# Cross attention: the context rows turned by VectorE from a second load instead of by TensorE

## What is computed

```python
def xattn(x, z, Wq, Wkv, Wo):          # x: 64 x 32 x 512, z: 64 x 257 x 256, 16 heads of 32
    Q = (x @ Wq.T).reshape(B, xN, 16, 32)
    KV = (z @ Wkv.T).reshape(B, zN, 2, 16, 32)
    K, V = KV[:, :, 0], KV[:, :, 1]
    attn = softmax(einsum('bqhd,bkhd->bhqk', Q, K) * SCALE, axis=-1)
    O = einsum('bhqk,bkhd->bqhd', attn, V).reshape(B, xN, 512)
    return O @ Wo.T
x = x + xattn(layernorm(x), ctx_512, ...)
```

## Time and profile before

| | |
|---|---|
| median of 3 runs | 1498.38 us (1495.2 to 1499.29) |
| span of the profiled execution | 1492.9 us, 39481 instructions |
| TensorE busy | 1434.5 us, 96% |
| VectorE busy | 1088.6 us, 73% |
| ScalarE busy | 807.5 us, 54% |
| GpSimd busy | 543.6 us, 36% |
| mean granted clock of TensorE | 0.990 |

### The profile page before, as it was taken

The page is one execution under the profiler, slowest core; times in us unless marked ns, Lnnn a source line. Parts: engine busy times, 40 slices in busy tenths (PEclk is TensorE's granted clock), DMA queues, the critical chain, the costliest instruction groups (busy, mean ns, idle before and its releaser), DMA issues. The chain is left out here.

```text
span 1492.9 us, 39481 instructions
## 1 busy us (share of the span) xinstructions
PE 1434.5 (96%) x14944; PEld 1281.3 (86%) x14944; DVE 1088.6 (73%) x1945; ACT 807.5 (54%) x1525; POOL 543.6 (36%) x810
## 2 busy tenths in 40 slices
PE   7999999999999999998999998799999999999998
PEld 6888888988888888887778786698999999999997
DVE  3676777767777677776667686797887878787785
ACT  4666666666666666654434434345555545555452
POOL 1222222221222222224866876453333333333232
PEclk9999999999999999999999999899999999999999
DMA  6301101000001100100011014179877878787871
GB/s 239 125 28 31 30 22 29 29 22 29 22 28 28 29 28 23 30 9 1 31 38 38 32 38 155 57 220 314 281 263 247 286 253 267 262 279 238 292 256 44
DMA packets 130734, 174.11 MB, mean 117 GB/s; under 512 B 16953, under 2 KB 89337, under 8 KB 130626
## 3 DMA queue, kind: packets, MB, share of 16 engines
q1 hardware_dynamic: 120242, 145.56, 30.1%
q0 software_dynamic: 10384, 27.05, 5.0%
HBM read 157.18 MB, written 19.06 MB: 118 GB/s over the span
## 5 line engine op out<-in xcount | busy, mean ns | idle before, releaser
L2229 DVE TENSOR_TENSOR split<-raw,split 128x1024 fp32r<-128x1024 f32 x204 | 242.3, 1220 | 7.2 <-ACT split L2169 6.0
L52 PE MATMUL bank<-split_xT,split 128*128 128x256 f32 x768 | 216.5, 282 | 0.4 <-DVE split L2229 0.2
L54 PE MATMUL bank<-split_xT,split 128*128 128x256 f32 x768 | 215.4, 281 | 0.0
L53 PE MATMUL bank<-split_xT,split 128*128 128x256 f32 x768 | 215.4, 280 | 0.0
L2169 ACT CAST split<-raw 128x1024 fp32r<-128x1024 f32 x202 | 203.2, 1048 | 6.9 <-DMA raw<-in_L_ffn_W_dram 3.2
L596 ACT ACTIVATE Pr<-xa_s,nmax 128x257 f32<-128x257 f32 x256 | 118.7, 473 | 124.9 <-DVE nmax L696 124.8
L2189 ACT ACTIVATE sl<-bank 128x256 f32<-128x256 f32 x115 | 44.2, 384 | 240.8 <-PE bank L54 223.5
L52 PE MATMUL xa_s<-split,split 128*128 128x258 f32 x512 | 150.5, 294 | 1.9 <-DVE split L628 1.9
L52 PEld LDWEIGHTS bank<-split_xT,split 128*128 128x128 f32 x768 | 144.9, 189 | 7.0 <-issue 2.8
L53 PEld LDWEIGHTS bank<-split_xT,split 128*128 128x128 f32 x768 | 145.0, 189 | 3.1
L53 PE MATMUL xa_s<-split,split 128*128 128x258 f32 x512 | 145.6, 284 | 0.0
(11 more groups left out here) (317 smaller groups left out, 3915.1 us busy)
## 6 DMA issues: line engine op xcount, KB each, us to landing
raw<-in_L_ffn_W_dram SPq DMA_DIRECT2D x207, 512.0 KB
raw<-in_ctx_dram SPq DMA_DIRECT2D x64, 256.0 KB, 2.6
out_dram<-x_res SPq DMA_DIRECT2D x16, 256.0 KB
xs<-xn SPq DMA_DIRECT2D x16, 256.0 KB
x_res<-in_x_dram SPq DMA_DIRECT2D x1, 3584.0 KB, 18.7
VL<-v_last_rows SPq DMA_DIRECT2D x128, 2.0 KB, 1.5
raw_o<-in_L_xattn_Wo_dram SPq DMA_DIRECT2D x1, 1024.0 KB, 6.4
raw_q<-in_L_xattn_Wq_dram SPq DMA_DIRECT2D x1, 1024.0 KB, 9.5
```

The lines of the kernel that those rows point to most:

```text
L52: pe.matmul(out, lh, rh, start=start, stop=False)
L53: pe.matmul(out, ll, rh, start=False, stop=False)
L54: return pe.matmul(out, lh, rl, start=False, stop=stop)
L2229: vW.done(dve.tensor_tensor(lo, raw, hi.bitcast(F32), ALU.subtract), f"p{c}{q}")
```

## The change

z comes to the core a second time, in 32x32 blocks. `load_blocks` brings a sequence in four transfers of 128-byte runs, so that the block of 32 keys and 32 features stands with its keys on the 32 partitions where its features shall end. VectorE then turns the blocks within each group of 32 partitions by two block transposes of 128x256 (`turn_z`, now on VectorE), into an SBUF buffer `zT`. `z_hi` and `z_lo` read `zT` instead of PSUM, and TensorE's turns are gone. The blocks have two buffers and `zT` one; they lie in the third weight slot. The weights of the self attention that were loaded there (wv, wo) are loaded at the end of the cross attention, each with a semaphore of its own that ScalarE waits for.

The transposes write whole runs of 32 keys, which makes the keys stand in another order along a row; `load_z` gives the rows of z the same order, in four transfers of 64 KB. The transposes stand on VectorE behind the second maximum (at j=0 also behind the masked copies, at j=2 behind the layer norm) and ahead of the reciprocal. The diff's core:

```diff
+        GRP = P // HD
+        zb = [lent.w2[:, n, :] for n in range(2)]
+        zb_got = [sem(f"zb_got{n}") for n in range(2)]
+        zT = lent.w13[:, 1, 0:2].rearrange("p k w -> p (k w)").rearrange("p (k c) -> p k c", k=KL)
+        def load_blocks(sp, s, n):
+            blocks = ctx_in[s, 0:LAST, :].rearrange("(i n) (k g e) -> i g (n k) e", i=HD, k=KL, e=HD)
+            for g in range(GRP):
+                sp.dma_start(zb[n][g * HD:(g + 1) * HD, :].rearrange("p (n e) -> p n e", e=HD), blocks[:, g]).then_inc(zb_got[n], 16)
+        def turn_z(dve, n, got, s):
+            dve.wait_ge(zb_got[n], got)
+            if not isinstance(s, int) or s:
+                dve.wait_ge(a_T, s)
+                dve.wait_ge(v_T, s)
+            for k in range(KL):
+                dve.transpose(zT[:, k].rearrange("p (c b i) -> p b c i", c=CH, b=BT),
+                              zb[n].rearrange("p (b c k e) -> p k b c e", b=BT, c=CH, k=KL)[:, k]).then_inc(v_ZT, 1)
         def load_z(sp, s, j):
-            sp.dma_start(z_in[j], ctx_in[s, 0:LAST, :].rearrange("(p c) l -> p c l", c=CH)).then_inc(z_got[j], 16)
+            rows = ctx_in[s, 0:LAST, :].rearrange("(i b c) l -> b i (c l)", i=HD, b=BT)
+            for b in range(BT):
+                sp.dma_start(z_in[j][b * HD:(b + 1) * HD].rearrange("p c l -> p (c l)"), rows[b]).then_inc(z_got[j], 16)
...
-                    for j in range(BT):
-                        load_z(sp, j, j)
+                    load_blocks(sp, 0, 0)
+                    load_z(sp, 0, 0)
+                    load_z(sp, 1, 1)
+                    load_blocks(sp, 1, 1)
...
                         if not first:
-                            sp.wait_ge(pe_T, s - BT + 1)
                             sp.wait_ge(g_Z, s - BT + 1)
                             load_z(sp, s, j)
+                        elif j >= 2:
+                            load_z(sp, s, j)
+                        if not (last and j >= 2):
+                            sp.wait_ge(v_ZT, KL * s + KL)
+                            load_blocks(sp, s + 2, j % 2)
...
+                sp.wait_ge(v_T, s_end)
+                weights.load_v(sp)
+                weights.load_o(sp)
...
-                        if not (last and j == BT - 1):
-                            turn_z(s + 1, (j + 1) % BT, i + (j + 1) // BT)
...
                 def z_hi(s):
-                    act.wait_ge(pe_T, s + 1)
-                    act.copy(zT_hi[:, :, 0:LAST], bank_z[:].rearrange("p (k q) -> p k q", k=KL)).then_inc(a_T, 1)
+                    act.wait_ge(v_ZT, KL * s + KL)
+                    act.copy(zT_hi[:, :, 0:LAST], zT).then_inc(a_T, 1)
...
-                    dve.tensor_tensor(zT_lo[:, :, 0:LAST], bank_z[:].rearrange("p (k q) -> p k q", k=KL),
+                    dve.tensor_tensor(zT_lo[:, :, 0:LAST], zT,
                                       zT_hi[:, :, 0:LAST].bitcast(F32), ALU.subtract).then_inc(v_T, 1)
...
                         if j == 2:
                             normalise(dve, i + 2)
+                        if not (last and j == BT - 1):
+                            turn_z(dve, (j + 1) % 2, 16 * GRP * (2 * i + (j + 1) // 2 + 1), s + 1)
                         dve.wait_ge(a_E, 4 * s + 4)
                         dve.reciprocal(rinv[:], rsum[:]).then_inc(v_R, 1)
...
                 high(0)
+                act.wait_ge(w.v_got, 16)
                 w.high(act, 2)
...
+                act.wait_ge(w.o_got, 16)
                 w.high(act, 3)
```

More of the change, by code:

```diff
@@ L82, in block_constants, with cross_attention @@
     return ident
-def cross_attention(nc, x_in, ctx_in, Wq, Wkv, Wo, x_res, ident, vlast_dram, spare,
+def cross_attention(nc, x_in, ctx_in, Wq, Wkv, Wo, x_res, ident, vlast_dram, spare, lent,
                     spare_x, held, weights, beside):
@@ L312, in cross_attention @@
         vl_got, vl_made, vl_split = sem("vl_got"), sem("vl_made"), sem("vl_split")
-        pe_T, pe_S, pe_PT, pe_U, pe_QK = (sem(n) for n in ("pe_T", "pe_S", "pe_PT", "pe_U", "pe_QK"))
+        pe_S, pe_PT, pe_U, pe_QK = (sem(n) for n in ("pe_S", "pe_PT", "pe_U", "pe_QK"))
         pe_PL, pe_O, pe_Q, pe_OP = (sem(n) for n in ("pe_PL", "pe_O", "pe_Q", "pe_OP"))
@@ L679, in add_residual @@
                     dve.tensor_tensor(x_res[:, i, :], bank_o[:], x_res[:, i, :], ALU.add).then_inc(v_OP, 1)
+                turn_z(dve, 0, 16 * GRP, 0)
                 z_lo(0)
@@ L745, in split_z @@
                 def split_z(s, j, i):
-                    pool.wait_ge(z_got[j], 16 * i + 16)
+                    pool.wait_ge(z_got[j], 16 * BT * i + 16 * BT)
                     need(pool, pe_U, s)
@@ L822, in __init__ @@
         self.got = ctx.enter_context(nc.semaphore("sa_w_got"))
+        self.v_got, self.o_got = (ctx.enter_context(nc.semaphore(n)) for n in ("sa_wv_got", "sa_wo_got"))
         self.loads = [(dst, src.rearrange("(k p) c -> p k c", p=P)) for dst, src in (
-            (self.q, wq), (self.down[:], w_down), (self.k, wk_up), (self.v, wv_up), (self.o, wo), (self.router[:], Wr))]
+            (self.q, wq), (self.down[:], w_down), (self.k, wk_up), (self.router[:], Wr))]
+        self.late_v, self.late_o = ((dst, src.rearrange("(k p) c -> p k c", p=P)) for dst, src in ((self.v, wv_up), (self.o, wo)))
         self.loads.append((self.rope[:], rope.rearrange("p (a d) -> p a d", a=2)))
@@ L842, in load, with load_v, load_o @@
             sp.dma_start(dst, src).then_inc(self.got, 16)
+    def load_v(self, sp):
+        sp.dma_start(*self.late_v).then_inc(self.v_got, 16)
+    def load_o(self, sp):
+        sp.dma_start(*self.late_o).then_inc(self.o_got, 16)
     def wait(self, eng):
@@ L2405, in perceiver_block @@
             cross_attention(nc, x.rearrange("b t c -> (b t) c"), ctx_512, xWq, xWkv, xWo, x_res, ident,
-                            v_last, slots[0], xg, held, weights, clear_slots)
+                            v_last, slots[0], slots[2], xg, held, weights, clear_slots)
             banks = Banks(nc, ctx)
```

4 lines of the change are left out of this document (2 added, 2 removed).

## The result

The changed kernel takes 1483.26 us (median of four runs, 1483.19 to 1484.38) against 1498.84 us for the kernel before (1495.20 to 1500.59): a ratio of 0.990, with an interval of 0.989 to 0.992. The forecast was 1483.0 us. The profiled execution took 1484.38 us, with a span of 1482.6 us against 1492.9 before.

The account below looks back on a forecast made before the run. TensorE's own work was taken to bound the cross attention. The loop's -16.1 us and the start's +0.5 gave -15.6, so 1498.4 became 1482.8, say 1483 us; range 1471 to 1497, with 1480 to 1488 at 0.60.

Parts of the forecast that it names:

- The loop: Cross attention tiles: -1.14 us for each of 13 middle tiles (-14.8), with tiles 0, 14 and 15 summing to -16.1.
- j=0: Sequence without a VectorE gap: U ends 0.68 us later, the values wait, 11.22 against 11.04 us, a loss of 0.18.
- the list of signs: What would show the forecast right, including TensorE waiting near 0.9 us for VectorE's U ahead of the values at j=0.
- The pair: Two 128x256 block transposes per sequence on VectorE: 0.42 us each, 0.68 on its path with overlap.
- the rival of slow transposes: VectorE transposes at the 128x512 price: pair 1.28 us instead of 0.68, about 5 us lost, 1493; chance 0.14.
- The step that j=3 would pay from 1.2 us on: VectorE at j=3: with cover gone, each 0.1 us of the pair over 1.2 costs 0.1.
- The start: SyncE ahead of the first barrier: twelve more issues at 0.6 to 0.96 us each, put at +0.5 us, range 0 to +4.
- Loads in the loop: SyncE and DMA engines: eight 64 KB loads per sequence instead of one of 256 KB, and late wv and wo, cost nothing.
- The rival of late blocks: The eight loads exceed a sequence; each us over 10 adds to each of 62 sequences, 1545 at 11 us; chance 0.07.
- The shared path: VectorE's low half of z and GpSimd's split block each other; z_lo wins, the split runs 0.5 us late, harmlessly.
- The rival's mechanism: GpSimd's split, if issued first, makes z_lo wait 2 us: +2.9 a tile, +38 in all, 1536; chance 0.09.
- The baseline: The median 1498.4 us from which -15.6 was subtracted, with 2 to 6 us taken to lie around the profiled span.

Follow-up runs that it names:

- e1_start: The changed kernel with only the first sequence's block load ahead of the first barrier, the other loads issued behind it: 1478.03 us.
- e7_loads4: The kernel before with the new loads, blocks read by nothing, TensorE still turning z, rows of z loaded four sequences ahead: 1503.47 us, recorded ratio 1.0035.
- e5_pool: The changed kernel with GpSimd allowed to begin its split of z's rows one step earlier, issued ahead of VectorE's low part of z: 1486.47 us.
- e4_early: The changed kernel with the transposes at j=0 moved to the end of j=3 of the tile before, behind the low part of z: 1479.78 us.
- e3_double: The changed kernel with each pair of transposes done twice, first into a buffer that nothing reads: 1496.83 us.

## Why the prediction came out right, point by point

- **The loop** (forecast -16.1, profile -18.1 with -16.5 in tiles 1 to 13). Every turn that was to be won at j=1, j=2 and j=3 was won. Tile 0 gave -0.85 (forecast -0.9), tile 14 -0.94 (-0.7), and the first three sequences of tile 15 +0.21 (+0.3). What follows them to the self attention took 1.2 us more, where the granted clock fell (0.77 and 0.81 from 662 to 670 us); in e1_start the same code at full clock took what it took before.
- **j=0** (forecast +0.18 each, measured +0.04 on average). The mechanism was right: no gap, U late, TensorE waits 0.60 us for it (the list of signs said 0.9, the sum's own numbers make 8.43 - (8.08 - 0.44) = 0.79). The size was off by 0.14: U ends at 8.25 and not 8.38, since the pair follows the masks with 0.08 overlap and the reciprocal takes 0.14 us behind a transpose instead of 0.18.
- **The pair** (forecast 0.42 each, 0.68 on the path). Measured 0.418 and 0.68. Strided reads cost nothing; the rival of slow transposes is out. The step that j=3 would pay from 1.2 us on was too strict: with 1.33 us it paid 0.04 instead of 0.13.
- **The start** (forecast +0.5, at most +4; measured +7.25). This is the step that failed, in two ways. The sum priced twelve more issues at 0.6 to 0.96 us and left the first four at their old 3.82 us. The twelve took 6.9 us, 0.57 each, but the first four, now transfers of 128-byte runs, took 7.80 in the same place. So SyncE ended at 23.01, the upper end of the 19 to 23 that the prediction worked out, while the +0.5 came from near the lower end, and TensorE's start in the kernel before was 18.99 and not 19.7: 4.5 us. And the clock was put at nothing: the longer wait for the barrier was followed by a slower granted clock, 2.7 us. A first barrier several us later stood among the signs of being wrong, and it came.
- **Loads in the loop** (forecast nothing). Shown by e7_loads4, to 0.05 us in 525. The rival of late blocks is out: in the changed kernel's trace the transposes are idle ahead of them once only, at the first barrier, and ScalarE doesn't stand for wv or wo.
- **The shared path.** GpSimd's first instruction waits as forecast (0.57 instead of 0.19 us), L647 stays at 0.68. The rival's mechanism was right. Its condition was not enough, as GpSimd came first in one sequence of four though it was issued ahead in all, and its price was too high (e5_pool).
- **The baseline.** I subtracted from a median whose spread I had not explained. The 2 to 6 us that I put around the span are 1.7 to 2.3. The profiled pair says -18.1 + 7.25 + 1.2 - 0.7, which is -10.3; the two pairs of medians say -15.6 and -11.6. The loop's underestimate and the draw covered the start's error, and that is why 1483.0 met 1483.3: the total was luck, the loop's mechanism was not.

## What to carry to other kernels

When work goes from the engine that bounds to one with gaps, walk the gaps step by step: it was free in three of four sequences and cancelled its whole gain in the fourth, which had no gap. Count every DMA that is issued ahead of a barrier at the price of its own form, and put there only what the first step needs. Before a difference of a few microseconds is explained, learn what the kernel's own runs differ by, and where.

## What the runs showed of the hardware that was not expected

- In the changed kernel an issue of 64 KB in 512 runs of 128 bytes took SyncE 1.95 us on average (1.3 to 2.7) in the first four, while the start's weights were landing, 0.65 in the four at 19.77 us, and 0.57 at the median over all; one of z's rows of the same size took 0.53 at the start and 0.32 at the median.
- VectorE stands 0.21 us for nothing that the profile shows, ahead of the maxima at j=0 of the first tile of a pair, in five iterations of the hardware loop of pairs. Each time a branch of the loop (COMPARE_BRANCH, here at 354.34) stands 0.5 us before in VectorE's own queue:

```profile
354.83 1.29 DVE L716 TENSOR_REDUCE nmax<-xa_s 128x2 f32<-128x514 f32 x2 [0.21 <-issue]
```

It was hidden before (j=0 took 11.04 to 11.05 us in every tile from 2 to 13); with VectorE on the path, j=0 is 0.12 to 0.20 us longer in every second tile from tile 4 on, and about 0.3 in e4_early and e3_double. Its cause was not tried, nor whether it makes up the whole of that.

- A GpSimd instruction on 128x1 elements, 0.19 us by itself, takes 0.57 us beside one of VectorE's instructions with two SBUF inputs (L647, 0.68 us) and 1.10 us beside another (L652, 1.22 us). Beside the old low part of z (L628), which has one input in PSUM, it took 0.19.
